# Other layouts for kv and the gram in a two-layer attention kernel: k and v as separate blocks, the gram with its sequences innermost

## The reference

```
x = x + window_attention(gn(x))        # shifted windows of 8 x 8, 16 heads of 16, cosine scores, bias, mask, softmax
x = x + axial_attention(gn(x))         # along the rows and along the columns of an image, summed
```

```
qkv  = x @ w_qkv;  q, k, v = split(qkv, 3)          # heads of 16 channels
dots = einsum('bhie,bhje->bhij', q, k) * d ** -0.5
out  = einsum('bhij,bhje->bhie', dots, v)           # linear in k and v
return out @ w_out
```

## Time and profile before

| what | us |
|---|---|
| median of 3 runs | 912.56 (911.0 to 913.3) |
| the profiled execution | 910.2 |
| its span, first to last instruction | 908.4 |
| TensorE matmuls busy | 846.0 |
| VectorE busy | 730.3 |
| ScalarE busy | 666.0 |
| GpSimd busy | 493.0 |

### The profile page before, as it was taken

How to read it: one execution, slowest core, us unless ns; L and a number is a source line. 1 busy time by engine, 2 the same in 40 slices (tenths; PEclk the granted TensorE clock), 3 DMA queues, 4 the chain that set the end, 5 groups by cost and what they waited for, 6 DMA issues and landing times.

```text
span 908.4 us, 45985 instructions
## 1 busy us (share of the span) xinstructions
PE 846.0 (93%) x20128; PEld 660.0 (73%) x20128; DVE 730.3 (80%) x1528; ACT 666.0 (73%) x1112; POOL 493.0 (54%) x366
## 2 busy tenths in 40 slices
PE   5478899999999999999999999999999999999865
PEld 3354677777878877777877777778787777777554
DVE  7879888888888988888888888888889888886431
ACT  3666677887777787887777878877778778777441
POOL 4545455565565565565565565655655655655321
PEclk9698999999999999999999999999999999999888
DMA  6201344434334444434334444343444443343433
GB/s 165 57 13 40 74 80 80 78 77 88 78 82 82 92 91 90 84 80 90 79 78 87 86 92 91 74 88 78 85 81 91 90 92 70 72 81 78 92 74 82
DMA packets 334431, 74.04 MB, mean 82 GB/s; under 512 B 282373, under 2 KB 333719, under 8 KB 334231
## 3 DMA queue, kind: packets, MB, share of 16 engines
q1 hardware_dynamic: 331728, 71.10, 37.8%
q10 hardware_dynamic: 2502, 0.01, 0.2%
HBM read 12.31 MB, written 8.40 MB: 23 GB/s over the span
## 4 chain that ended last, share of the span: by engine, by line
PE 76%; SPq 7%; DVE 6%; issue 4%; DMA 3%; ACT 3%; POOL 1%; POOLq 0%; DVEq 0%; ACTq 0%
PE ps L518 20%; PE ps L588 15%; PE ps L631 9%; PE ps L620 7%; PE ps L609 6%; PE ps L535 4%; SPq L439 4%; PE ps L621 4%; PE ps L550 3%; PE ps L559 3%; PE ps L568 3%; SPq L429 2%; DMA gram_wide<-gram 2%; PE ps L658 2%; PE ps L652 1%
## 5 line engine op out<-in xcount | busy, mean ns | idle before, releaser
L1147 POOL TENSOR_TENSOR kv<-kv,kv 128x1024 f16<-128x1024 f32 x64 | 137.0, 2141 | 90.0 <-ACT kv L882 84.6
L930 ACT ACTIVATE probs<-probs 128x1024 f32<-128x1024 f32 x64 | 67.8, 1059 | 91.9 <-DVE probs L1407 89.7
L620 PEld LDWEIGHTS ps<-q,gram_wide 128*128 128x128 f16 x2048 | 107.5, 97 | 13.2 <-DMA gram_wide<-gram 5.4
L620 PE MATMUL ps<-q,gram_wide 128*128 128x32 f16 x2048 | 111.6, 177 | 5.4 <-DMA gram_wide<-gram 5.3
L1152 POOL TENSOR_TENSOR stat<-stat,small 128x2 f32<-128x2 f32 x64 | 43.3, 693 | 133.1 <-DVE stat L1326 125.3
L1352 DVE SCALAR_TENSOR_TENSOR gram<-ps,small,gram 128x512 f16<-128x512 f32 x128 | 94.5, 793 | 23.0 <-ACT gram L899 19.8
L621 PE MATMUL ps<-q,gram_wide 128*128 128x16 f16 x2048 | 110.7, 169 | 0.0
L621 PEld LDWEIGHTS ps<-q,gram_wide 128*128 128x128 f16 x2048 | 106.2, 97 | 0.4
L518 PE MATMUL ps<-xn,w_q 128*128 128x256 f16 x768 | 97.4, 278 | 7.0 <-POOL xn L1147 7.0
L899 ACT ACTIVATE gram<-ps,small 128x512 f16<-128x512 f32 x128 | 95.3, 817 | 8.0 <-PE ps L609 8.0
L1147 POOL TENSOR_TENSOR xn<-xn,xn 128x512 f16<-128x512 f32 x64 | 74.9, 1170 | 47.7 <-ACT xn L919 47.7
(11 more groups left out here) (122 smaller groups left out, 1961.2 us busy)
## 6 DMA issues: line engine op xcount, KB each, us to landing
gram_wide<-gram SPq DMA_DIRECT2D x256, 128.0 KB, 3.1
v_wide<-kv SPq DMA_DIRECT2D x512, 32.0 KB, 2.3
x_in<-x SPq DMA_DIRECT2D x32, 128.0 KB, 2.4
x_in<-x SPq DMA_DIRECT2D x64, 64.0 KB, 2.3
out<-y_out SPq DMA_DIRECT2D x32, 128.0 KB, 2.2
out<-y_out SPq DMA_DIRECT2D x64, 64.0 KB, 2.0
x<-L_conv_w_qkv SPq DMA_DIRECT2D x1, 768.0 KB, 4.4
y_out<-L_conv_w_out SPq DMA_DIRECT2D x2, 256.0 KB, 4.8
```

Source lines behind the costliest of these rows:

```text
L620: pe.matmul(dst.rearrange("p (t i) -> p t i", t=2), high, q1[a][:, :, cols], start=True, stop=False)
L930: act.activation(part, part, ACT.Exp).then_inc(probs_ready[g], 1)
L1147: return pool.tensor_tensor(dst, whole, high, ALU.subtract)
```

## The change

`kv` gets an axis for its kind (k or v) outside of precision and token half. The v part of a partition is then one run of 1,024 elements (2 KB) instead of four of 256. `token_high` and `token_low` write both kinds through `by_kind`, and `gram_matmuls` reads k from kind 0.

`gram` and `gram_wide` get the order channel of v, sequence, precision. `gram_wide` has the quarter of its block-diagonal outermost. Each partition of a quarter is then one run of 4 KB in source and destination, instead of 32 runs of 128 bytes. The instructions of `gram_half` write their 512 numbers still sequence by sequence, now with 64 elements (128 bytes) between two channels and 2 elements between two sequences. The weights of `axial_out` take 128 columns at a step of 64 elements.

```diff
--- before.py
+++ after.py
@@ -161,11 +161,11 @@
         x1 = sb("x1", [P, 4, HALF])
         q1 = [sb(f"q1_{a}", [P, 2, HALF], F16) for a in range(2)]
         kv32 = [sb(f"kv32_{a}", [P, 2, HALF]) for a in range(2)]
-        kv = [sb(f"kv_{a}", [P, 2, 2, 2 * D], F16) for a in range(2)]
+        kv = [sb(f"kv_{a}", [P, 2, 2, 2, D], F16) for a in range(2)]
         v_wide = [sb(f"v_wide{a}", [P, 4, 2, 2, D], F16) for a in range(2)]
-        gram_both = sb("gram", [P, 2, G * SEQ, 32, 2], F16)
+        gram_both = sb("gram", [P, 2, 32, G * SEQ, 2], F16)
         gram = [gram_both[:, a] for a in range(2)]
-        gram_wide = [sb(f"gram_wide{a}", [P, G * SEQ, 4, 32, 2], F16) for a in range(2)]
+        gram_wide = [sb(f"gram_wide{a}", [P, 4, 32, G * SEQ, 2], F16) for a in range(2)]
         o1_32 = [sb(f"o1_32_{a}", [P, HALF]) for a in range(2)]
         o1 = [sb(f"o1_{a}", [P, 2, HALF], F16) for a in range(2)]
         y = sb("y", [P, HALF])
@@ -329,7 +329,7 @@
 
         def gram_half(a, head, t):
 
-            return gram[a][:, :, DH * head:DH * head + DH, t]
+            return gram[a][:, DH * head:DH * head + DH, :, t].rearrange("p e s -> p s e")
 
         def gram_psum(a, head, img):
 
@@ -342,6 +342,10 @@
         def in_columns(ap):
 
             return ap.rearrange("p (g c r) -> p g c r", r=SIDE, c=SIDE)
+
+        def by_kind(ap):
+
+            return ap.rearrange("p t (k n) -> p k t n", k=2)
 
         def by_token(ap, t, a):
 
@@ -426,8 +430,8 @@
                 reach(sp, gram_lo[a], img)
                 for q in range(4):
                     rows = slice(32 * q, 32 * q + 32)
-                    sp.dma_start(gram_wide[a][rows, :, q].rearrange("p s e t -> p s (e t)"),
-                                 gram[a][rows].rearrange("p s e t -> p s (e t)")).then_inc(gram_spread[a], 16)
+                    sp.dma_start(gram_wide[a][rows, q].rearrange("p e s t -> p (e s t)"),
+                                 gram[a][rows].rearrange("p e s t -> p (e s t)")).then_inc(gram_spread[a], 16)
 
             def spread_v_rows(a, img):
 
@@ -436,8 +440,8 @@
                 reach(sp, kv_lo[a], img)
                 for s in range(8):
                     rows = slice(SEQ * s, SEQ * s + SEQ)
-                    sp.dma_start(v_wide[a][rows, s % 4].rearrange("p l t n -> p (l t) n"),
-                                 kv[a][rows, :, :, D:2 * D].rearrange("p l t n -> p (l t) n")).then_inc(v_spread[a], 16)
+                    sp.dma_start(v_wide[a][rows, s % 4].rearrange("p l t n -> p (l t n)"),
+                                 kv[a][rows, 1].rearrange("p l t n -> p (l t n)")).then_inc(v_spread[a], 16)
 
             def store_image(img):
                 reach(sp, y_copied, img)
@@ -606,7 +610,7 @@
                                 for h in range(2):
                                     rows = slice(64 * h, 64 * h + 64)
                                     dst = ps[32 * q:32 * q + 32, G_BANK[a](img) + h, at:at + P]
-                                    last = pe.matmul(dst.rearrange("p (s e) -> p s e", e=32), kv[a][rows, kp, t, own],
+                                    last = pe.matmul(dst.rearrange("p (s e) -> p s e", e=32), kv[a][rows, 0, kp, t, own],
                                                      v_wide[a][rows, :, vp, t, own], start=(n == 0), stop=(n == 2))
                 last.then_inc(gram_done[a], 1)
 
@@ -616,7 +620,7 @@
                     cols = slice(s * SEQ, (s + 1) * SEQ)
                     dst = ps[:, O_BANK[a](img) + s // SEQ, (s % SEQ) * 2 * SEQ:(s % SEQ + 1) * 2 * SEQ]
                     at = gram_place(*divmod(s, SEQ))
-                    high, low = (gram_wide[a][:, at, :, :, gp].rearrange("p h e -> p (h e)") for gp in range(2))
+                    high, low = (gram_wide[a][:, :, :, at, gp].rearrange("p h e -> p (h e)") for gp in range(2))
                     pe.matmul(dst.rearrange("p (t i) -> p t i", t=2), high, q1[a][:, :, cols], start=True, stop=False)
                     last = pe.matmul(dst[:, 0:SEQ], low, q1[a][:, 0, cols], start=False, stop=True)
                 last.then_inc(o1_done[a], 1)
@@ -879,7 +883,7 @@
                 reach(act, kv1_proj[a], img)
                 reach(act, v_spread[a], previous(img), 128)
                 reach(act, gram_done[a], previous(img))
-                act.activation(kv[a][:, 0], ps[:, KV_BANK[a](img):KV_BANK[a](img) + 2, :], ACT.Copy).then_inc(kv_hi[a], 1)
+                act.activation(kv[a][:, :, 0], by_kind(ps[:, KV_BANK[a](img):KV_BANK[a](img) + 2, :]), ACT.Copy).then_inc(kv_hi[a], 1)
 
             def token_copy(a, img):
                 reach(act, kv1_proj[a], img)
@@ -1129,7 +1133,7 @@
         def _(pool):
 
             pool.memset(v_diag[:].rearrange("p a b c d -> p (a b c d)"), 0.0).then_inc(zeroed, 1)
-            pool.memset(gram_wide[0][:].rearrange("p s q e t -> p (s q e t)").bitcast(F32), 0.0).then_inc(wide_zeroed, 1)
+            pool.memset(gram_wide[0][:].rearrange("p q e s t -> p (q e s t)").bitcast(F32), 0.0).then_inc(wide_zeroed, 1)
             pool.wait_ge(first_in, 16 * 3)
 
             def zero_v_wide():
@@ -1165,7 +1169,7 @@
                 reach(pool, kv_copied[a], img)
                 reach(pool, gram_done[a], previous(img))
                 reach(pool, v_spread[a], previous(img), 128)
-                low(kv[a][:, 1], kv32[a][:], kv[a][:, 0]).then_inc(kv_lo[a], 1)
+                low(kv[a][:, :, 1], by_kind(kv32[a][:]), kv[a][:, :, 0]).then_inc(kv_lo[a], 1)
 
             def qk_low(img):
                 reach(pool, qk_hi, img)
@@ -1234,7 +1238,7 @@
 
         @block.vector
         def _(dve):
-            dve.memset(gram_wide[1][:].rearrange("p s q e t -> p (s q e t)").bitcast(F32), 0.0).then_inc(wide_zeroed, 1)
+            dve.memset(gram_wide[1][:].rearrange("p q e s t -> p (q e s t)").bitcast(F32), 0.0).then_inc(wide_zeroed, 1)
             dve.wait_ge(first_in, 16 * 3)
 
             def cap_scale():
```

## The result

The changed kernel takes 1,499.33 us (1,497.98 to 1,501.25, four runs), the kernel before, on the same chip, 912.93 (911.0 to 914.02): a ratio of 1.6425, 95% interval 1.6379 to 1.6472. It is slower by 586 us. The direction was forecast; the size (955 us, up to 1,032) was not.

A forecast was written before the change was run, and what follows sets the result against it. TensorE's own work was taken as the steady bound. The profiled 910.2 us, + 49 for weight loads, - 8 for transfers, 0 for the rest, made 951, 953.6 as a timed median, stated as 955; range 904 to 1,032 us.

The forecast's parts named there:

- Part 1: Gram and v transfers in 4 and 2 KB runs: 0 to 14 us off the ends, 8 taken, nothing in steady steps.
- The v groups, at 2 us each, give 6 us: SyncE queue in the tail: three groups of 16 v issues shorten, at 0.64 us per issue, saving 6 us.
- Part 2: kv written as k, then v by ScalarE and GpSimd: 0 us.
- Part 3: ScalarE and VectorE gram writes at 128 bytes: 0.4 us more per instruction, bounds 0 to 0.92, net nothing on the path.
- Both stay below 25.6: Work per step with longer gram writes: ScalarE 21.7 us and VectorE 23.4, under TensorE's step of 25.6.
- Net nothing on the path: From gram_done to landing: 1.6 us more write latency, offset by 2.1 us less for the transfer behind it.
- Part 4: axial_out weight columns read at 128 bytes: 12 ns more per load, bounds 0 to 28, 4,096 loads, 49 us.
- with the granted clock still 1.00: Sign of being right: TensorE's granted clock stays 1.00 from 200 to 800 us, with a step of 27.1 us.
- C: Rival at axial_out's loads: each pair goes from 25.2 to 50 to 53 ns, about 1,013 us; chance 0.27.
- B: Rival: loads are free, VectorE's gram instructions gain 0.92 us each and it becomes the bound, 931 us; chance 0.10.
- A: Rival: reads are free and coarser transfers show in the SyncE tail and last waits, 905 us; chance 0.14.
- D: Rival: nothing to be seen, with free reads, fixed issue cost and ends unmoved, 912 us; chance 0.07.

The follow-up runs named there:

- B: Changed kernel with only the coarser transfers, gram written and axial_out weights taken at the old 4-byte step: 909.73 us against 912.07 for the kernel before.
- A: Kernel before with only the kv half of the change (k and v as separate blocks): 912.11 us against 910.03, ratio 1.0007.
- G: Kernel before, ScalarE's gram write at steps of 4 to 128 bytes by image, VectorE's at 4, 124 and 128: one execution of 1,142 us, for durations.
- C: Changed kernel with axial_out weights at the old 4-byte step, gram still written at 128 bytes: 1,364.03 us, ratio 1.499 to the kernel before.
- J: Changed kernel with weights at 4 bytes and gram written at 128 bytes in one direction only: direction 0 alone 1,170.17 us, direction 1 alone 1,149.2.
- F: Whole changed kernel, same layouts, gram instructions going channel by channel (SBUF written at 4 bytes, PSUM read at 128): 1,277.33 us, ratio 1.4016.
- D: Changed kernel with the gram written at the old 4-byte step, axial_out weights still at 128 bytes: 1,277.42 us, ratio 1.4016 to the kernel before.
- E: Kernel with only the weight loads at 128 bytes, each axial_out matmul streaming 128 columns instead of 32 and 16: 1,163.84 us, ratio 1.2763.
- H: Kernel before with axial_out's weights taken at steps of 4 to 128 bytes, varied by image: one execution of 1,072 us, for distances between matmuls.

## Why the prediction was wrong

*What bounds the kernel.* Right: TensorE's own work, with transfers that hide. B shows that all that finer packets cost was 2.5 us.

*Part 1 (transfers).* Right in sign, mis-sized: 8 us was forecast, 2.5 measured. The step that failed is "The v groups, at 2 us each, give 6 us", from 0.64 us for each issue with its gap: the three v groups together became 0.6 us shorter in B, since the issue's cost hardly depends on its runs.

*Part 2 (kv).* Right: 0 (A).

*Part 3 (gram written across).* Wrong, and the first large miss: + 0.4 us per instruction, bounds 0 to 0.92, was taken from a read. Measured + 1.87 on ScalarE and + 1.89 on VectorE, twice the bound. A read of fp32 at 64 bytes, 1.7 times as long as in a row, says nothing of a 2-byte write at 128, which is 3.3 times its time at 4 bytes (G). What followed from it failed as well: "Both stay below 25.6" (VectorE has 30 us of work in a step, so it would be the bound by itself in C) and "Net nothing on the path". Four such instructions add 7.5 us of latency between `gram_matmuls` of direction 0 and those of direction 1, where the trace before has 0.5 to 0.9 us between the last write and the matmuls, and hold up what is queued behind them in direction 1 (J). In the changed kernel this is 222 us (F). There, beside the long loads, VectorE's 30.4 us stay under TensorE's 38.1, and the kernel stood still all the same, by waits in the order of the queues.

*Part 4 (loads across).* The mechanism was right, the size was not. The step that failed is the reading share of 11 to 12.6 ns, doubled: "I take 12". Measured: + 62 ns per load in D, + 63 in the changed kernel (medians of 64 blocks), five times as much and above my dear end of 28. The slope between loads of 32 and of 128 columns was taken from loads at full rate (one with 64 rows, one with 128) and did not bound a slow one. In E this term is 252 us, where I had 49. The two rules of the Trainium skill: Advanced Engine Details and Errata, section SBUF Cachelines, has lines of 16 bytes and two hits per line for full rate. The trace agrees in where the level begins: the loads of H take 60.3 ns at 16 bytes and stay there to 124, the writes of G likewise. It does not agree at 8 bytes, where a line is hit twice: 33.3 ns instead of 25.2 for a load, 1,399 instead of 818 for a write. TensorE: Matmul & The Clock Gate, section Weight-path perf modes, admits column steps up to 1,024 elements for the fast load. The prediction read that as loads that keep their time; the Trainium skill gives no time for a step there. At 64 elements the loads took 62 ns more: the measurement decides.

*The clock.* Missing altogether: "with the granted clock still 1.00" stood among the signs of being right. It is 0.81, and worth 114 us with the loads alone (D less E). Of the 586 us then: 252 loads, 114 the clock that they cost, 222 writes, nearly all by waits. The three were taken off one after another (1,499, 1,277, 1,164, 911); the order matters, since alone the writes cost 454 (C).

*Rivals.* C (the loads pay in full) was nearest and still 480 us short. B had VectorE's longer writes as the matter, but at half their price and as the bound of a kernel with free loads. I had treated the two as alternatives, and both prices came due. A and D, with free reads, are out.

Open: why 128 bytes cost a load 27 ns more than 124 or 132; whether it is the columns' distance or that of other parts of one load was not told apart. What VectorE's read across costs beside its write was not measured alone, and the 222 us are split only by the busy and idle time of the rows above, not by a run.

## What to carry to other kernels

A layout that makes a transfer's runs longer moves a step from the transfer to the engines, and engines pay per element: count the instructions that read or write that tile element by element before the packets. Keep neighbours of a 2-byte operand 4 bytes apart on the side of SBUF that is written or loaded as a weight (8 bytes already cost 1.7 times for a write and 1.3 times for a load here), and turn the order of a write, not its layout, if the other side is PSUM. A price that the trace has no row for needs a range that its nearest row doesn't limit, above all when it stands 4,096 times on the bound.

## What the runs showed of the hardware that I had not expected

- Writing 512 fp16 numbers to SBUF: 818 ns at a step of 4 bytes, 1,399 at 8, 2,561 to 2,685 from 16 to 128, all on ScalarE. VectorE takes 2,591 at 128, reading one operand at the same step. fp32 at 128 bytes: 1,139 and 1,114.
- Reading PSUM with 128 bytes between neighbours instead of 4: 828 ns against 816 on ScalarE, 841 against 849 on VectorE.
- Loading 128 columns as weight: 25.2 ns between matmuls at 4 bytes, 33.3 at 8, 60 to 62 from 16 to 124, 87.4 at 128, 60.6 at 132.
- A TensorE whose matmuls the profile shows busy all the time was granted 0.82 of its clock with 32 and 16 columns streamed behind each long load, and 1.00 with 128: more work took 114 us less.
